# A three-engine hand-over in a four-layer kernel: GpSimd's scales and weight pieces at other places, statistics buffers of their own, first pairs shared with ScalarE

## The chip, the cores and the metric

The kernel runs on one core of a Trainium2 chip. Its time is device time in microseconds, the median of several executions; lower is better. Five engines work side by side and are ordered by semaphores alone: TensorE (PE) multiplies, VectorE (DVE), ScalarE (ACT) and GpSimd (POOL) do everything between the matmuls, and SyncE (SP) issues the transfers. Every engine carries out its own instructions in the order in which the kernel lists them; an instruction whose semaphore isn't there holds back all that stand behind it on that engine.

## The reference

Four layers on x of shape 8 x 256 x 256 (batches, tokens, features), each with a layer norm ahead of it and a residual around it:

```python
x = x + attention(layernorm(x))   # 16 heads in 4 groups, causal, softmax, projection
x = x + ternary_linear(layernorm(layernorm(x), gamma, beta))  # weights -1, 0, 1
x = x + linear_attn(layernorm(x))
x = x + gated_ffn(layernorm(x))

# linear_attn: Q, K, V = split(X W_in + b_in); Q, K get a rotary embedding
A = sum over tokens of (K / |K|) * V
Y = (A * Q) W_out + b_out
# and adds the normalised X itself

# gated_ffn: integer weights minus 128, times a scale per row
out = (silu(x Wg) * (x Wu)) Wd
```

All values are float32. Products are made of rounded float32 parts: an operand is split into a high part (the rounded copy) and a low part (what is left), and most products are three matmuls: high by high, high by low, low by high. So nearly every tile is needed twice, as a high half that ScalarE copies out of the matmul's bank and as a low half that VectorE gets by a subtraction.

## The kernel before

**Stages.** The eight batches of 256 tokens go through attention one after the other (`batch(n, last)` on every engine; n = 0 is written out, 1 to 6 are a loop, 7 is written out). Within a batch, j counts 8 pairs of heads. The ternary layer of batch n - 1 and the statistics for the linear layer lie within the attention of batch n; the ternary layer of the last batch lies within the linear layer. That layer is `linear(n)` for n = 1 to 7, all written out, and the gated layer is `gated(m, ...)` over four pairs of batches with six tiles of the hidden dimension each, in a loop for the middle two. The opening (before `batch(0, False)`) is an order written out by hand, since the weights arrive meanwhile.

**A pair of heads.** TensorE makes the scores of pair j + 2 while the probabilities of pair j are transposed. VectorE's `row_max` adds the causal mask to the first 128 rows' diagonal block (line 1528), then takes sum and minimum in four custom reductions (line 1532). ScalarE's `exps` makes the exponentials with their row sums (line 1141). VectorE inverts the sums (line 1548); `normalise` multiplies the probabilities of head 0 on GpSimd (line 521) and of head 1 on VectorE (line 1557). For the very first pair VectorE also does the second rows of head 0 (line 1554). TensorE transposes them (lines 751 and 754), ScalarE and VectorE split them (`pT_hi`, line 1103, and `pT_lo`, line 1486), and `attend` and `out_project` use them. `q_hi`, `q_lo`, `v_hi`, `v_lo`, `o_hi` and `o_lo` split other tiles by the same two lines. `late_hi` and `late_lo` split weights in the first batch.

**GpSimd's other work.** It makes the low halves of the gated layer's weights in eight pieces (`gated_weights_lo`, line 538; GU0 and GU1 with four parts each), takes the variances to the power -1/2 (`inv_std`, `inv_std_twice`), makes the scales of the linear layer in seven small operations (`linear_scale(n)`, lines 490 to 499), adds bias rows to the residual (`add_row`, line 455: `linear_bias`, `ternary_bias`), and in the linear layer does the rotary embedding's sine products (line 468), the sums (lines 478 and 485) and the inverse norm of k (line 508), which ScalarE's `weigh` (line 1337) waits for.

**A step of the linear layer.** On TensorE, `linear(n)` is: k projection of batch n, output product of batch n - 2 (`linear_out`, line 940), transposes of the normalised batch n + 1 (line 659), `linear_sum(n - 1)` (line 927), q projection of batch n. VectorE applies the norm (`linear_apply`, line 1731), makes the q products (lines 1761 and 1764), copies k with its bias (line 1744), makes its cosine products (line 1752), adds the output product to x (`add_bank`, line 1720), splits the transposed tile (line 1486) and reduces the token sums to A (`linear_sum`, line 1776). ScalarE scales q by A to y (`linear_y`, line 1353). GpSimd's `q_rotate` and `k_inverse` stand between these. In step 2 VectorE normalises the last batch for the ternary layer (`ternary_apply`, line 1709) at the end; in steps 3 and 5 it splits the down projection's weights (line 1816).

**Hand-over.** The gated layer's first two batches are normalised within steps 7 and 8 of this order: `ln_moments` (lines 1469 and 1473) on VectorE, `inv_std` (lines 444 and 446) on GpSimd, `gated_apply` (line 1480), transposes, `gated_x_hi` and `gated_x_lo` (lines 1280 and 1830). All calls of `ln_moments` share the buffers `stats`, `moments`, `variance` and `rstd`, and are counted: call NB + b is the gated batch b. After the last step ScalarE does `linear_y(NB - 1)`, then the first silu (line 1390), before which an activation table is loaded. A flag that says whether any low half of the gated weights is other than zero is made of four sums (`sum_gated_lo`, `sum_down_lo`, line 1245, on ScalarE); it picks two matmuls instead of three per product in the gated layer of this run.

## Time and profile before

| what | value |
|---|---|
| median of 3 runs (lowest to highest) | 582.9 us (582.8 to 583.08) |
| the profiled execution's own time | 582.94 us |
| its span | 581.1 us |
| TensorE matmuls, weight loads | 564.4 us, 532.3 us |
| VectorE, ScalarE, GpSimd | 469.1 us, 370.8 us, 220.9 us |

The span runs from the first instruction of the program to the last one, and the time has 1.84 us around it. "Busy" means that an instruction of the engine was under way; the matmuls are pipelined, so TensorE's 564.4 us isn't TensorE at its peak. An idle piece of an engine is put down to the instruction whose semaphore came last. By the timeline the opening is 0 to about 60 us (the first batch), attention goes on until about 445 us, the linear layer's steps until about 504 us, the gated layer until about 574 us.

### The profile page before, as it was taken

How to read it: one execution, taken by the hardware profiler on the slowest of the kernel's cores; microseconds unless marked ns; L12 is line 12 of the kernel's file. 1: busy time of each engine (PE TensorE's matmuls, PEld its weight loads, DVE VectorE, ACT ScalarE, POOL GpSimd, SP SyncE). 2: the span in 40 equal slices, each digit the busy share in tenths (PEclk: the TensorE clock that was granted, in tenths of full speed). 3: DMA queues.
4: the chain of work that ended last, by engine and by line, in shares of the span. 5: the costliest groups of instructions: out<-in, count | busy, mean ns of one | idle time of the engine just before them, and what ended most of it. 6: DMA issues, size and time to landing. Idle time of an engine off the chain costs nothing.

```text
span 581.1 us, 12867 instructions
## 1 busy us (share of the span) xinstructions
PE 564.4 (97%) x4131; PEld 532.3 (92%) x4131; DVE 469.1 (81%) x1476; ACT 370.8 (64%) x1035; POOL 220.9 (38%) x325
## 2 busy tenths in 40 slices
PE   8899999999999999999999999999999898899995
PEld 8799999999999999999999999999998797788884
DVE  5789789778878987797789778977877997878875
ACT  5896656656755756576567657557877776654452
POOL 3773224233223422332233233323446798503320
PEclk9999999999999999999999999999999998999998
DMA  8806000000000000000000000000000000001001
GB/s 324 293 1 227 2 1 3 1 1 0 0 0 0 0 0 0 0 0 0 0 0 0 0 0 0 0 0 1 1 1 2 1 2 0 2 0 37 25 30 57
DMA packets 9152, 14.71 MB, mean 25 GB/s; under 512 B 1568, under 2 KB 6688, under 8 KB 9120
## 3 DMA queue, kind: packets, MB, share of 16 engines
q1 hardware_dynamic: 9120, 14.30, 6.9%
q8 instruction: 18, 0.29, 0.2%
q14 instruction: 14, 0.11, 0.1%
HBM read 12.20 MB, written 2.10 MB: 25 GB/s over the span
## 4 chain that ended last, share of the span: by engine, by line
PE 83%; DVE 7%; POOL 4%; ACT 3%; issue 2%; POOLq 0%; DVEq 0%; ACTq 0%
PE bank L649 67%; PE bank L735 5%; PE bank L751 5%; PE bank L754 2%; PE bank L659 2%; DVE raw L1764 1%; PE bank L864 1%; ACT prob L1141 1%; PE bank L1048 1%; POOL qkv L468 1%; POOL prob L508 1%; DVE prob L1532 1%; ACT raw L1330 0%; DVE raw L1761 0%; POOL qkv L485 0%
## 5 line engine op out<-in xcount | busy, mean ns | idle before, releaser
L521 POOL TENSOR_SCALAR prob<-prob,rowinv 128x256 f32<-128x256 f32 (+1 forms) x127 | 96.3, 771 | 273.3 <-DVE rowinv L1548 273.3
L649 PE MATMUL bank<-xT,big 128*128 128x256 f32 x984 | 129.7, 284 | 0.1
L649 PEld LDWEIGHTS bank<-xT,big 128*128 128x128 f32 x984 | 123.4, 192 | 1.0 <-issue 0.2
L1141 ACT ACTIVATE prob<-prob,negmax 128x128 f32<-128x128 f32 (+1 forms) x256 | 112.8, 444 | 9.5 <-DVE negmax L1532 9.5
L649 PE MATMUL bank<-wp,oT 128*128 128x256 f32 x768 | 102.5, 283 | 0.2
L649 PEld LDWEIGHTS bank<-wp,oT 128*128 128x128 f32 x768 | 96.8, 190 | 1.2 <-DVE oT L1486 0.7
L1103 ACT ACTIVATE qT<-bank 128x512 fp32r<-128x512 f32 x68 | 40.6, 597 | 72.8 <-PE bank L649 72.7
L649 PE MATMUL bank<-pT,v 128*128 128x512 f32 (+1 forms) x384 | 80.0, 343 | 0.1
L649 PEld LDWEIGHTS bank<-pT,v 128*128 128x128 f32 x384 | 63.1, 189 | 9.5 <-issue 0.5
L1486 DVE TENSOR_TENSOR pT<-bank,pT 128x512 fp32r<-128x512 f32 (+1 forms) x128 | 65.1, 550 | 3.1 <-ACT pT L1103 3.0
L1103 ACT ACTIVATE pT<-bank 128x512 fp32r<-128x512 f32 (+1 forms) x128 | 55.2, 483 | 12.1 <-PE bank L751 10.0
L1486 DVE TENSOR_TENSOR qT<-bank,qT 128x512 fp32r<-128x512 f32 x68 | 46.8, 688 | 16.7 <-ACT qT L1103 16.7
L1486 DVE TENSOR_TENSOR oT<-bank,oT 128x512 fp32r<-128x512 f32 x64 | 44.0, 688 | 15.7 <-ACT oT L1103 15.0
L649 PE MATMUL bank<-kT,qT 128*128 128x256 f32 x384 | 56.2, 282 | 0.0
L649 PEld LDWEIGHTS bank<-kT,qT 128*128 128x128 f32 x384 | 50.2, 190 | 0.0
L1532 DVE CUSTOM_DVE_ANT_0 prob<-bank,mask 128x256 f32<-128x256 f32 x128 | 48.6, 416 | 0.0
L1141 ACT ACTIVATION_READ_ACCUMULATOR prob<-prob,negmax 128x1 f32 x256 | 48.5, 190 | 0.0
L735 PE MATMUL bank<-kT,qT 128*128 128x256 f32 x256 | 46.1, 302 | 1.5 <-DVE negmax L1532 1.2
L649 PE MATMUL bank<-wp,big 128*128 128x512 f32 (+1 forms) x176 | 45.3, 398 | 0.8 <-DVE wp L1830 0.7
L1103 ACT ACTIVATE oT<-bank 128x512 fp32r<-128x512 f32 x64 | 37.2, 581 | 4.4 <-PE bank L649 4.4
L751 PE MATMUL bank<-ident,prob 128*128 128x128 f32 x256 | 38.3, 272 | 0.0
L649 PEld LDWEIGHTS bank<-wp,big 128*128 128x128 f32 x176 | 31.6, 189 | 7.1 <-DVE wp L1830 1.1
(180 smaller groups left out, 965.1 us busy)
## 6 DMA issues: line engine op xcount, KB each, us to landing
raw<-in_wq SPq DMA_DIRECT2D x4, 512.0 KB, 7.0
raw<-in_wp SPq DMA_DIRECT2D x4, 512.0 KB, 7.3
x<-in_x SPq DMA_DIRECT2D x7, 256.0 KB, 7.0
out<-x SPq DMA_DIRECT2D x7, 256.0 KB, 2.1
raw<-in_w_gu SPq DMA_DIRECT2D x2, 640.0 KB, 5.1
raw<-in_w_in SPq DMA_DIRECT2D x1, 768.0 KB, 4.6
raw<-in_w_down SPq DMA_DIRECT2D x1, 640.0 KB, 6.8
raw<-in_wk SPq DMA_DIRECT2D x1, 512.0 KB, 3.8
```

The lines of the kernel that those rows point to most:

```text
L468: m = pool.tensor_tensor(k_sin[q][:, :, e, :], k[:, :, 1 - e, :], sin[:, :, e, :], ALU.mult)
L508: pool.tensor_tensor(xw[n % 2][:, :, D:D + 1], k_bound[:, :].rearrange("p (t o) -> p t o", o=1), exponent[:, 0:ST].rearrange("p (t o) -> p ...
L521: m = pool.tensor_scalar(prob[:, j % 2, 0, a:b], prob[:, j % 2, 0, a:b], rowinv[:, j % 2, r:r + 1], None, ALU.mult)
L649: m = pe.matmul(out, lhs(a), rhs(b), start=first and i == 0, stop=last and i == len(passes) - 1, skip_group_check=True)
L659: m = pe.transpose(out[:, k * S + t * P:k * S + (t + 1) * P], src[:, t, k * P:(k + 1) * P], ident[:])
L735: m = pe.matmul(bS0[:, i * S:(i + 1) * S], qT[:, a, i, 0:P], kT[:, :, g, 0:P], start=a == 0, stop=a == 1, skip_group_check=True)
L751: m = pe.transpose(bT0[:, i * S + r * P:i * S + (r + 1) * P], prob[:, j % 2, i, r * P:(r + 1) * P], ident[:])
L754: m = pe.transpose(bT1[:, i * P:(i + 1) * P], prob[:, j % 2, i, 2 * P:3 * P], ident[:])
L1103: act.activation(out, src, ACT.Copy).then_inc(done, 1)
L1141: m = act.activation(prob[:, j % 2, i, a:b], prob[:, j % 2, i, a:b], ACT.Exp, scale=-1.0, bias=negmax[:, 2 * i + r:2 * i + r + 1], accum_o ...
L1486: dve.tensor_tensor(out, src, f32(hi), ALU.subtract).then_inc(done, 1)
L1532: return dve.tensor_tensor_reduce(prob[:, j % 2, i, a:b], src, other, -SCALE, -MASKED, ALU.add, ALU.min, negmax[:, 2 * i + r:2 * i + r + 1])
```

## The change

GpSimd: all four pieces of GU0 are made at j = 4 of the last attention batch, and after them the linear scales of batch 6 (before: two pieces there, two more at j = 6, the scales in step 3 of the linear layer). Three pieces of GU1 follow at j = 6 (before: one there, two in step 4); the fourth stays in step 5. The scales of batch 7 move from the start of step 5 to the end of step 4. The statistics for these scales move with them on VectorE: those of batch 6 go from step 2 to j = 5 of the last attention batch.

Second gated batch: its statistics use the buffers of the ternary layer (`t_stats`, `t_moments`, `t_variance`, `t_rstd`), which are free by then, in functions of their own, at the end of step 6; its normalisation moves into step 7, ahead of `linear_sum(6)`; TensorE transposes it ahead of `linear_sum(7)`. VectorE's tail after step 7 has another order, and the shared calls are renumbered. The ternary normalisation of step 2 moves from the end to after the q products.

Opening: ScalarE normalises head 1 of the first pair and splits its transposed probabilities ahead of the exponentials of pair 1. VectorE's `row_max` is in two functions, and the first (the masked add) of pairs 1 and 2 stands ahead of an inversion.

Tail: both multiplications of the last batch's scales stand ahead of both adds.

```diff
 # GpSimd
+            def gated_inv_std():
+                pool.wait_ge(s_fvar, NB + 1)
+                pool.tensor_tensor(t_rstd[:, :], t_variance[:, :], exponent[:, 0:ST], ALU.pow).then_inc(s_frs, 1)
 # batch(n, last)
                         if j == 4:
-                            gated_weights_lo(GU0, 0)
-                            gated_weights_lo(GU0, 1)
+                            for part in range(4):
+                                gated_weights_lo(GU0, part)
+                            linear_scale(NB - 2)
                         if j == 6:
-                            gated_weights_lo(GU0, 2)
-                            gated_weights_lo(GU0, 3)
-                            gated_weights_lo(GU1, 0)
+                            for part in range(3):
+                                gated_weights_lo(GU1, part)
 # linear(n)
-                if n == 5:
-                    linear_scale(NB - 1)
                 if n > 0:
                     q_rotate(n - 1)
...
-                if n >= NB - 2:
-                    inv_std(n + 2)
+                if n == NB - 2:
+                    inv_std(NB)
...
-                if n == 3:
-                    linear_scale(NB - 2)
                 if n == 4:
-                    gated_weights_lo(GU1, 1)
-                    gated_weights_lo(GU1, 2)
+                    linear_scale(NB - 1)
                 if n == 5:
                     gated_weights_lo(GU1, 3)
+                if n == NB - 2:
+                    gated_inv_std()
 # TensorE, linear(n)
                 if n == NB - 1:
+                    gated_transpose(1)
                     linear_sum(n)
-                    gated_transpose(1)
                     linear_out(n - 1)
 # ScalarE
+            def normalise_first():
+                act.wait_ge(s_ri, 1)
+                for r, (a, b) in enumerate(((0, P), (P, 3 * P))):
+                    m = act.activation(prob[:, 0, 1, a:b], prob[:, 0, 1, a:b], ACT.Copy, scale=rowinv[:, 0, 2 + r:3 + r])
+                m.then_inc(s_pn1, 1)
...
+                if n == 5:
+                    sum_down_lo(1)
                 if n == NB - 2:
                     sum_gated_lo(GU1)
-                    sum_down_lo(1)
...
             v_hi(0, 0)
+            normalise_first()
             late_hi(3)
             q_hi(0, 2)
+            pT_hi(0, 0)
             exps(0, 1)
 # VectorE: row_max(n, j) is now row_max_first(n, j), the masked add, and
 # row_max_rest(n, j), the four reductions
             q_lo(0, 1)
+            row_max_first(0, 1)
             invert_sums(0, 0)
             normalise(0, 0)
             v_lo(0, 0)
-            row_max(0, 1)
+            row_max_rest(0, 1)
             q_lo(0, 2)
+            pT_lo(0, 0, 0)
+            pT_lo(0, 0, 1)
+            row_max_first(0, 2)
             invert_sums(0, 1)
             normalise(0, 1)
             batch(0, False)
 # in batch(0) at j == 0: row_max_rest(0, 2) ahead of q_lo(0, 3), in place of
 # row_max(0, 2) behind it
 # batch(n, last) at j == 5
                             linear_apply(1)
                             o_lo(n, j)
+                            linear_moments(NB - 2)
 # linear(n)
                     q_products(n - 1)
+                    if n == 2:
+                        ternary_apply(NB - 1)
...
-                    if n >= NB - 2:
-                        ln_moments(n + 2, n + 2 - NB)
+                    if n == NB - 2:
+                        ln_moments(NB, 0)
                     add_bank(n - 2, bY, s_lo, s_lres, s_la)
                     linear_x_lo(n + 1, (n + 1) % 2) if n + 1 < NB else gated_x_lo(0)
+                    if n == NB - 1:
+                        gated_apply(1)
                     linear_sum(n - 1)
...
-                if n == 2:
-                    ternary_apply(NB - 1)
-                    linear_moments(NB - 2)
...
+                if n == NB - 2:
+                    gated_moments()
                 if n == NB - 1:
-                    gated_apply(1)
 # after step 7
+            gated_x_lo(1)
+            linear_sum(NB - 1)
             q_products(NB - 1)
-            linear_sum(NB - 1)
-            gated_x_lo(1)
 # tail
             for t in range(ST):
                 dve.tensor_tensor(scaled[1][:, t, :], ...)
+            for t in range(ST):
                 dve.wait_ge(s_gsc, b + t + 1)
                 dve.tensor_tensor(x_tile(b, t), x_tile(b, t), scaled[1][:, t, :], ALU.add).then_inc(s_gl, 1)
```

`gated_moments()` is `ln_moments` and the variance plus epsilon for batch 1 with the ternary buffers: two `bn_stats`, two `bn_aggr` and one `tensor_scalar`.

## Rows read from the trace of the kernel before

**Rows 1.** The page: each engine's busy time, its share of the span, instructions

```profile
PE 564.4 (97%) x4131; PEld 532.3 (92%) x4131; DVE 469.1 (81%) x1476; ACT 370.8 (64%) x1035; POOL 220.9 (38%) x325
```

**Rows 2.** Waits of TensorE: who for whom, us in total, times, longest

```profile
PE bank L940 <- ACT raw L1353: 2.2, 1, 2.2
...
PE bank L659 <- DVE y L1709: 1.8, 1, 1.8
PE bank L735 <- DVE negmax L1532: 1.2, 1, 1.2
PE bank L649 <- DVE wp L1830: 0.7, 1, 0.7
PE bank L659 <- DVE xn L1480: 0.5, 1, 0.5
```

**Rows 3.** Windows of 4 us: stretch, busy by engine, clock, DMA share, GB/s

```profile
484.00:488.00 4.00, 3.32 (x8) 2.56 (x9) 3.94 (x6) 1.97 (x5) 2.38 (x3) 0.62 0.00 0
```

**Rows 4.** Timeline of the opening: start, us, engine, line, tiles, idle before

```profile
16.26 0.49 ACT L1141 ACTIVATE prob<-prob,negmax 128x256 f32<-128x256 f32 x1
...
18.24 0.72 DVE L1557 TENSOR_SCALAR prob<-prob,rowinv 128x128 f32<-128x128 f32 x2
...
26.20 0.41 DVE L1528 TENSOR_TENSOR prob<-bank,mask 128x256 f32<-128x256 f32 x1
...
27.87 0.71 PE L735 MATMUL bank<-kT,qT 128*128 128x256 f32 x4 [1.20 <-DVE negmax L1532]
```

**Rows 5.** Timeline of the last attention batch

```profile
430.90 1.86 POOL L538 TENSOR_TENSOR big<-raw,big 128x352 fp32r<-128x352 f32 x2
...
433.06 0.73 DVE L1731 TENSOR_SCALAR xn_b<-x,linear_negated_mean,linear_rstd 128x256 f32<-128x256 f32 x2
...
435.47 1.02 DVE L1486 TENSOR_TENSOR pT<-bank,pT 128x512 fp32r<-128x512 f32 x2 [1.08 <-ACT pT L1103]
...
437.70 0.66 DVE L1557 TENSOR_SCALAR prob<-prob,rowinv 128x128 f32<-128x128 f32 x2
437.76 1.65 POOL L521 TENSOR_SCALAR prob<-prob,rowinv 128x128 f32<-128x128 f32 x2 [5.00 <-DVE rowinv L1548]
```

**Rows 6.** Timeline of the linear layer's steps

```profile
458.79 0.74 DVE L1676 BATCH_NORM_STATS2 linear_stats<-x 128x6 f32<-128x256 f32 x2
...
458.95 1.29 POOL L455 TENSOR_TENSOR x<-x,biases 128x512 f32<-128x512 f32 x1 [0.56 <-DVE y L1709]
...
459.74 0.98 DVE L1731 TENSOR_SCALAR xn<-x,linear_negated_mean,linear_rstd 128x256 f32<-128x256 f32 x2
...
474.29 0.89 ACT L1353 ACTIVATE raw<-qkv,A_sb 128x256 f32<-128x256 f32 x2
...
474.84 1.67 DVE L1731 TENSOR_SCALAR xn<-x,linear_negated_mean,linear_rstd 128x256 f32<-128x256 f32 x2
...
475.36 1.89 PE L940 MATMUL bank<-raw 128*128 128x256 f32 x8
...
483.97 1.93 DVE L1731 TENSOR_SCALAR xn_b<-x,linear_negated_mean,linear_rstd 128x256 f32<-128x256 f32 x2 [1.64 <-ACT prob L1337]
...
484.68 3.55 PE L940 MATMUL bank<-raw 128*128 128x256 f32 x8 [2.17 <-ACT raw L1353]
```

**Rows 7.** Timeline of the hand-over to the gated layer

```profile
492.13 1.60 DVE L1480 TENSOR_SCALAR xn<-x,moments,rstd 128x256 f32<-128x256 f32 x2 [0.86 <-POOL rstd L446]
...
502.34 0.98 DVE L1764 SCALAR_TENSOR_TENSOR raw<-bank,q_bias,rope 64x256 f32<-64x256 f32 x2
...
504.19 0.91 ACT L1353 ACTIVATE raw<-qkv,A_sb 128x256 f32<-128x256 f32 x2 [1.18 <-DVE A_sb L1776]
...
510.61 0.68 DVE L1851 TENSOR_TENSOR kT<-raw,kT 128x512 fp32r<-128x512 f32 x1
...
512.13 1.12 PE L649 MATMUL bank<-big,kT 128*128 128x256 f32 x8
```

**Rows 8.** Timeline of the tail

```profile
574.96 1.25 DVE L1983 TENSOR_TENSOR x<-x,qkv 128x256 f32<-128x256 f32 x1
```

More of the change, by code:

```diff
@@ L1577, in batch @@
                     if first:
+                        row_max_rest(n, 2)
                         q_lo(n, 3)
-                    if j < J - 2 or not last:
+                    elif j < J - 2 or not last:
                         row_max(*ahead(n, j, 2))
@@ L1981, in _ @@
                 dve.tensor_tensor(scaled[1][:, t, :], bD[1][:, t * D:(t + 1) * D], biases[:, 2, :], ALU.mult).then_inc(s_gsc, 1)
+            for t in range(ST):
                 dve.wait_ge(s_gsc, b + t + 1)
```

37 lines of the change are left out of this document (30 added, 7 removed).

## The prediction

> **What bounds the kernel now.** I read the page's busy times first: TensorE has work under way for 564.4 us of a span of 581.1 [rows 1], so a change that takes no matmul away can only win what TensorE waits. The waits of TensorE come next [rows 2]: 2.2 us in one piece for ScalarE's scaled y, 1.8 for VectorE's ternary xn, 1.2 for a row maximum in the opening, 0.7 for the low half of a transposed tile and 0.5 for a normalised tile at the hand-over to the gated layer; that for the constants at the start, which the change doesn't touch, and pieces under 0.3 us are left out here. Then the windows: after the 2.2 us wait the granted clock is 0.62 over 484 to 488 us, that is the 1.2 GHz level for most of that stretch, against 1.00 elsewhere [rows 3]. The reader sees the price beside it: the same eight matmul instructions take 3.55 us there and 1.89 one layer step earlier [rows 6], so the wait costs 2.2 + 1.7 = 3.9 us, and 0.2 more in the transposes behind it. The 1.8 us wait left the clock alone. Everything together is 6.4 us of waits and 1.9 us of clock, about 8.3 us, and the timeline around each wait says who is late. All steps are set against this execution: 582.94 us, 1.84 around its span; the median of the runs is 582.9, so nothing is to be shifted.
>
> **Opening (first pairs).** Removed from VectorE's path: the two normalisations of pair 0's second head, 0.72 us, and the masked add of 0.41 us in each of two row maxima, which moves into time in which VectorE waited for exponentials. Added to ScalarE: the same two normalisations; its exponential of the wider shape takes 0.49 us, so both some 0.8 to 0.9 us [rows 4]. VectorE reaches the second row maximum about 1.1 us sooner. The query tile of pair 2 now hangs on ScalarE, which does it after the normalisations and a weight copy: it comes 0.3 to 0.5 us sooner at most, and the exponentials of pair 1 start some 0.3 us later than at present. Following the order from there (low halves of pair 0's transposes, inversion, normalisation, v, then the rest of the third row maximum, 1.2 us of four reductions), the maximum that began at 26.20 is complete near 25.8 instead of 27.7, and TensorE's scores at 27.87 wait for the low half of the fourth query tile, near 26.5. TensorE's own work would let it start there at 26.5. Bounds: 0.2 us, if ScalarE's queue is what ends last, and 1.4, the wait with the sliver before it. I take 1.2, for VectorE's row is the one that ended last.
> The Trainium skill (Perfetto Trace Analysis, Optimizing Scalar/DVE Operations) holds that an operation which either engine can do is faster on VectorE where a performance mode exists, and that one moves it only if VectorE is saturated. The rows agree on the durations (0.72 against some 0.9) and not on the path: VectorE carries four tiles that TensorE waits for. By the rule the opening would give nothing, and the sum would be 1.2 us higher.
>
> **Last attention batch.** GpSimd stands idle for 5.00 us before its last normalisation at 437.76; two pieces of the gated weights take 1.86 us before that idle time [rows 5]. Two pieces more (1.9 us) and one set of linear scales (2.0) are put into it: 3.9 of 5.00 us. The scales wait for the moments of tile 6, which now stand on VectorE behind the normalised tile and the low half of o: 1.0 us, the pair of statistics as at 458.79 and a quarter for the aggregation [rows 6]. The idle time before VectorE's transposed probabilities at 435.47 is 1.08 us, so alone the moments would just fit. But VectorE's tensor_scalar on a 256-wide tile suffers from GpSimd's pieces: two take 0.73 us alone at 433.06 and 1.67 when they meet two pieces at 474.84 [rows 5, 6]. With the pieces 3 and 4 at 432.7 to 434.6, the three such operations at 432.8 to 433.8 lose 0.9 to 1.3 us. The probabilities then begin 0.9 to 1.3 us late, and TensorE's attend, which reads them, with them; short waits for VectorE in the same batch, under 0.3 us each, close in exchange. Behind the waiting scales on GpSimd is its last normalisation, which starts about 1.0 us late, when TensorE is late too. Bounds: 0 (the pieces don't meet those operations) and 1.3. I take +0.7.
> The Trainium skill (SBUF — State Buffer, Who interferes with whom) says that GpSimd and a two-port VectorE operation hold their shared ports for whole instructions and the other fully blocks. At 437.70 two VectorE normalisations lost only 0.12 us beside GpSimd's 1.65 us pair, so here the trace shows both behaviours. By full blocking this part costs 1.3, by the mild one 0.2.
>
> **Ternary layer's last tile.** VectorE's ternary normalisation moves ahead of k_copy, which takes away TensorE's 1.8 us wait. The tile steps behind it get later by 0.9 us (0.73 and one meeting with GpSimd's q_rotate). What is late next: GpSimd has two residual adds of 1.29 us one behind the other, the second no longer waiting for VectorE, and VectorE's linear_apply(4) meets both. It ends near 460.8, as now (459.74 + 0.98), and q products, k copy, k_squares, the transposed tile and the scaled y follow at today's times. TensorE's linear_out starts at 475.36 with y ready at 475.18 (474.29 + 0.89) [rows 6]; a TensorE that arrives 1.8 us early waits there instead. Bounds: 0 and -1.8. I take 0.
>
> **The wait for the scaled y.** Taken out of GpSimd's linear steps: two pieces (1.9 us by their length in [rows 5]) and one set of scales (some 2 us); the last set of scales follows the residual add directly. VectorE's apply at 474.84 then meets the add alone and gains 0.4 us. GpSimd's rotation, sine products and inverse, on which ScalarE's weighing and y wait, start 1.5 to 2 us sooner. y takes 0.89 us and ended with the wait, at 484.6; the queue gives it back 2.2 to 2.4 us, so it is ready near 482.3, and TensorE was free at 484.68 - 2.17 = 482.5 [rows 6]. So the 2.2 us wait and the 1.9 us of clock go, 4.1 us on TensorE. VectorE's chain, however, gains only what its next normalisation gains: it waited for the weighed x until 483.97 and then met an add and a piece (1.93 us) [rows 6]; the piece is still there, so it ends near 483.8 instead of 485.9, 2.1 us sooner. TensorE waits on that chain at the next k projection and y. Bounds: -2.1 (VectorE's chain decides) and -4.1 (TensorE decides). I take -2.1, because VectorE, ScalarE and GpSimd hand each tile around within one layer step and the margin at 475.36 was 0.2 us.
>
> **Second gated batch and hand-over.** The statistics of batch 1 (1.2 us on VectorE, 0.7 on GpSimd) move into VectorE's 0.86 us wait before 492.13; the normalisation there was held up to 1.60 us by an add and loses its excess, so they cost nothing [rows 7]. The normalisation of batch 1 moves ahead of linear_sum(6), and TensorE transposes it ahead of linear_sum(7). This takes away the waits of 0.5 and 0.3 us, and the low half that ended the 0.7 us wait comes 2.4 us sooner. What is late next is the tail: q products (0.98 us for two of three instructions, 1.45 for all) now stand behind the low half of the second transposed tile and the last linear_sum, so they and GpSimd's rotation (0.75) put the last y at about 505.5 in today's frame instead of 504.19. Behind y on ScalarE are the activation table's load and the first silu, and behind these the first low half of the hidden tile, which ends at 511.3, 7.1 us after y's start; TensorE's first down projection at 512.13 needs it [rows 7]. 505.5 + 7.1 = 512.6, so y's delay comes out there at +0.5 us net. Bounds: -1.5 (the waits just go) and +1.3 (y's whole delay). I take +0.5.
>
> **Tail.** The multiplication of the last tile runs beside the first add (1.25 us, slowed by GpSimd) instead of behind it: 0.41 us of multiplication leaves the end, of which the store's issue can use 0.2 to 0.4 [rows 8]. I take -0.3. The lo sum moved a step earlier on ScalarE finds its input ready and lies in idle time, and GpSimd's renumbered calls change no work: 0.
>
> **Sum.** -1.2 + 0.7 + 0 - 2.1 + 0.5 - 0.3 = -2.4 us: 582.94 - 2.4 = 580.5 us. Its own range, from the bounds that don't need another mechanism: 579.0 to 582.0.
>
> **Rivals.**
> (a) TensorE decides, not the chain of the other three. For it: VectorE is busy for 81% only, and two of its idle pieces in these steps are there because of the stalls themselves. Against it: the 0.2 us margin. Then -1.2 + 0.3 - 1.8 - 4.1 + 0 - 0.3 = -7.1: 575.8 us; halfway outcomes lie at 577 to 579.
> (b) The change gives nearly nothing: ScalarE becomes the bound of the opening (-0.2), the last batch costs its 1.3, the 2.2 us wait shrinks but reappears at the next y (-2.1), hand-over +0.5, tail 0: -0.5, 582.4 us. For it: ScalarE and VectorE are both full in the opening. Part of it is that the earlier statistics don't bring the second gated batch forward at all.
> (c) Slower. The one mechanism is VectorE's queue in the last batch: the moments that stand before the transposed probabilities. If the pieces and the statistics together hold the attend back by 2.2 us or more, the length of wait after which the clock fell at 484.68, the level of 1.2 GHz costs 1.9 on top, +4.1 in all. The other parts give -1.2 - 2.1 - 0.3 = -3.6, and the hand-over, whose last y hangs on the same VectorE, takes its upper bound of +1.3: 582.94 - 3.6 + 4.1 + 1.3 = 584.7 us. It decides from a wait of 2.2 us on; below that the sum stays under 582.94. Against it: I find 1.3 us at most for that wait.
>
> **Numbers.** Likeliest case 0.48, (a) with its halfway outcomes 0.27, (b) 0.15, (c) 0.10. A measurement of this kernel can tell a change of about 0.2%, 1.2 us, from none, so faster is below 581.7. The likeliest case gives 0.43 of that, (a) 0.27, (b) 0.02: faster 0.72. Slower is over 584.1: 0.08. Same 0.20. The range that holds it 8 times in 10 leaves out the slower case and the far end of (a): 576.5 to 582.8.
>
> **What would show it.** In the profile after, the wait of TensorE for VectorE's y near 459 is gone and a new one stands near the output product of step 5 (then 0 is right) or not (then (a)). The windows show a granted clock of 1.00 through the linear steps. The scores at 27.87 start near 26.6. In the last batch the attend that follows VectorE's row at 435.47 starts 0.9 to 1.3 us later against the projection before it, with VectorE's applies near 1.7 us instead of 0.73. The first down projection waits over 1 us, with the table load later against the gate projection than now. The prediction is wrong if the linear steps give over 4 us, or if the last batch costs over 1.5.

## Result and profile after

The changed kernel takes 580.42 us in the median of 5 runs (580.01 to 580.6); the kernel before takes 583.08 (582.8 to 583.26) beside it. The ratio is 0.9956, with an interval of 0.9944 to 0.9968. A second measurement on another chip gives 580.04 us and 0.9942 (0.9927 to 0.9957). The profiled execution has 580.42 us and a span of 578.6, so 2.5 us of span went.

The page of the changed kernel, busy times. TensorE does the same 4131 matmuls in 1.7 us less busy time than in [rows 1]; this is the clock, which had cost the output product of step 6 1.66 us (3.55 against 1.89 in [rows 6]). The other engines are where they were.

```profile
PE 562.7 (97%) x4131; PEld 530.6 (92%) x4131; DVE 469.3 (81%) x1475; ACT 370.7 (64%) x1037; POOL 220.5 (38%) x324
```

Waits of TensorE in the changed kernel (columns as in [rows 2]; the line numbers have moved, so L661 is L659 of before, L651 is L649):

```profile
PE bank L661 <- DVE xn L1865: 1.3, 1, 1.3
PE bank L651 <- DVE kT L1895: 1.2, 1, 1.2
PE bank L651 <- DVE qT L1498: 1.2, 2, 0.9
PE bank L651 <- DVE pT L1498: 1.2, 1, 1.2
PE bank L737 <- DVE qT L1498: 0.5, 2, 0.3
```

Four of the five waits of [rows 2] are gone. The fifth, 0.5 us for the second gated batch's xn, has grown to 1.3 at its new place, and two more single waits of over a microsecond have come, for kT and pT. All of them are for VectorE, and each is in a stage that the change gave more work or another order. The window in which the clock had been 0.62 [rows 3], and the stretch in which the output product of step 6 now lies, in the changed kernel:

```profile
484.00:488.00 4.00, 3.23 (x21) 2.81 (x19) 3.88 (x11) 1.70 (x6) 3.09 (x6) 1.00 0.00 0
...
480.00:484.00 4.00, 3.96 (x27) 3.38 (x26) 3.99 (x7) 3.49 (x9) 3.21 (x3) 1.00 0.00 0
```

To see where the 2.5 us come from, I compare the starts of the same TensorE instructions in both traces. "Against the loop" means: the shift of that start, less the shift of the transposes that stand at 289.75 us before and at 287.86 after, in the middle of the steady loop. This takes out the start of the execution, which scatters: the first transposes of probabilities (19.22 before, 19.06 after) lie between 18.70 and 20.02 us in the fourteen traces of this case. Every number in the table is the difference of two starts in the timelines.

| kernel | opening | attend, last batch | output product, step 5 | output product, step 7 | first down | last matmul | first transposes to last matmul |
|---|---|---|---|---|---|---|---|
| changed | -1.73 | +1.07 | +1.05 | -1.71 | -0.53 | -0.58 | -2.31 |
| changed, again (e7) | -1.73 | +1.04 | +1.01 | -1.76 | -0.59 | -0.73 | -2.46 |
| e1 opening only | -1.71 | -0.01 | +1.57 | -0.38 | +0.70 | +0.48 | -1.23 |
| e9 all but the opening | -0.02 | +1.06 | +1.06 | -1.74 | -0.56 | -0.65 | -0.67 |
| e2 ternary tile back | -1.72 | +1.08 | +0.95 | -2.28 | -1.11 | -1.26 | -2.98 |
| e3 weight pieces back | -1.72 | +1.06 | +1.06 | +0.10 | +1.28 | +1.14 | -0.58 |
| e4 tail order back | -1.72 | +1.09 | +1.03 | -1.76 | -1.82 | -1.91 | -3.63 |
| e5 statistics sooner | -1.73 | +0.12 | +0.10 | -2.67 | -1.49 | -1.63 | -3.36 |
| e6 pieces split | -1.72 | +0.51 | +0.62 | -2.17 | -0.98 | -1.10 | -2.82 |
| e8 two (e2, e4) | -1.74 | +1.07 | +0.96 | -2.29 | -2.35 | -2.46 | -4.20 |
| e10 three (e2, e4, e5) | -1.78 | +0.13 | +1.61 | -2.29 | -2.36 | -2.49 | -4.27 |
| e11 four (and e6) | -1.77 | +0.49 | +0.47 | -2.73 | -2.82 | -2.82 | -4.59 |
| e12 five | -1.75 | +0.48 | +2.03 | -1.89 | -2.66 | -2.80 | -4.55 |

The output products of steps 5, 6 and 7 are those that start at 475.36, 484.68 and 493.24 us in the kernel before. "Opening" is the shift of the loop against the first transposes; the last column is the opening and the last matmul together. The columns between are cumulative: the step from one to the next is the cost of the stage between them. For the changed kernel the stages are: opening -1.73, last attention batch +1.07, ternary tile -0.02, wait for y -2.76, hand-over +1.18, rest -0.05. The sum is -2.31; the first transposes were 0.16 sooner and the end behind the last matmul 0.04 shorter, which makes -2.51. Each row is one execution; the changed kernel's two agree within 0.15 us in every column.

The rows of the changed kernel behind these stages. Opening, answering to [rows 4]: the two normalisations that ScalarE took over, and the scores that stood at 27.87:

```profile
17.97 0.79 ACT L1152 ACTIVATE prob<-prob,rowinv 128x128 f32<-128x128 f32 x2
...
25.96 0.50 PE L737 MATMUL bank<-kT,qT 128*128 128x256 f32 x2 [0.32 <-DVE qT L1498]
```

Last attention batch, answering to [rows 5]:

```profile
429.01 3.74 POOL L543 TENSOR_TENSOR big<-raw,big 128x352 fp32r<-128x352 f32 x4
...
430.71 1.24 DVE L1578 TENSOR_SCALAR prob<-prob,rowinv 128x128 f32<-128x128 f32 x2
431.87 1.35 DVE L1754 TENSOR_SCALAR xn_b<-x,linear_negated_mean,linear_rstd 128x256 f32<-128x256 f32 x2
433.15 0.68 DVE L1498 TENSOR_TENSOR oT<-bank,oT 128x512 fp32r<-128x512 f32 x1
433.75 0.74 DVE L1699 BATCH_NORM_STATS2 linear_stats<-x 128x6 f32<-128x256 f32 x2
434.52 0.25 DVE L1704 BATCH_NORM_AGGREGATE linear_moments<-linear_stats 128x2 f32<-128x6 f32 x2
434.68 0.99 DVE L1498 TENSOR_TENSOR pT<-bank,pT 128x512 fp32r<-128x512 f32 x2
```

Two things stand ahead of the copy of pT: the statistics (433.75 to 434.68, 0.93 us), and the stretching of two pairs of VectorE's normalisations beside GpSimd's run of four pieces (1.24 and 1.35 us; the normalising pair takes 0.54 us at 432.61 before the change, the apply 0.73 in [rows 5]). Together 2.2 us; 1.08 us of idle time was there to take them. TensorE's attend at 435.49 waits 1.21 us.

Linear steps, answering to [rows 6]. The output product of step 6 starts without a wait, and TensorE waits later, at the k projection of step 7:

```profile
480.02 1.08 DVE L1841 SCALAR_TENSOR_TENSOR big<-raw,big 128x768 fp32r<-128x768 int32 x1
...
480.24 2.02 POOL L460 TENSOR_TENSOR x<-x,biases 128x512 f32<-128x512 f32 x1
...
481.02 2.34 DVE L1754 TENSOR_SCALAR xn_b<-x,linear_negated_mean,linear_rstd 128x256 f32<-128x256 f32 x2
...
481.40 1.97 PE L942 MATMUL bank<-raw 128*128 128x256 f32 x8
...
488.10 1.70 PE L651 MATMUL bank<-big,qT 128*128 128x256 f32 x12 [0.87 <-DVE qT L1498]
```

Hand-over, answering to [rows 7]: the last y, the load of the activation table behind it, the low half of the hidden tile and the first down projection:

```profile
502.56 0.91 ACT L1362 ACTIVATE raw<-qkv,A_sb 128x256 f32<-128x256 f32 x2 [3.66 <-POOL qkv L490]
...
503.49 1.28 ACT L1400 ACT_TABLE_LOAD   x1
...
508.98 0.68 DVE L1895 TENSOR_TENSOR kT<-raw,kT 128x512 fp32r<-128x512 f32 x1
...
509.71 1.22 PE L651 MATMUL bank<-big,kT 128*128 128x256 f32 x8 [1.24 <-DVE kT L1895]
```

Tail, answering to [rows 8]: both additions as one group, and the last stores on SP's queue; the last line is the second of the two stores in the line above it.

```profile
572.70 1.38 DVE L2032 TENSOR_TENSOR x<-x,qkv 128x256 f32<-128x256 f32 x2
573.49 0.37 SPq L421 DMA_DIRECT2D out<-x  x1
573.91 0.96 SPq L424 DMA_DIRECT2D out<-x  x2
574.42 0.44 SPq L424 DMA_DIRECT2D out<-x  x1
```

The same last store in the kernel before:

```profile
577.03 0.34 SPq L424 DMA_DIRECT2D out<-x  x1
```

### The profile page after: what moved, and what is told of

The parts are those of the page before. It is cut to its first block, busy times and chain, and to the rows that moved or that the text cites. A ratio compares the mean times of both kernels' runs of the same rounds, so it can differ in the third digit from the quotient of the medians.

```text
span 578.6 us, 12867 instructions
## 1 busy us (share of the span) xinstructions
PE 562.7 (97%) x4131; PEld 530.6 (92%) x4131; DVE 469.3 (81%) x1475; ACT 370.7 (64%) x1037; POOL 220.5 (38%) x324
## 4 chain that ended last, share of the span: by engine, by line
PE 80%; DVE 10%; ACT 5%; issue 3%; POOL 1%; DMA 0%; DVEq 0%; SPq 0%; POOLq 0%
PE bank L651 65%; PE bank L737 5%; PE bank L753 4%; PE bank L756 2%; PE bank L661 2%; ACT prob L1143 1%; PE bank L866 1%; DVE raw L1787 1%; DVE xn_b L1754 1%; DVE prob L1552 1%; DVE qkv L1767 1%; ACT raw L1339 1%; DVE pT L1498 1%; ACT big L1116 0%; DVE oT L1498 0%
## 5 line engine op out<-in xcount | busy, mean ns | idle before, releaser
L651 PE MATMUL bank<-xT,big 128*128 128x256 f32 x984 | 129.7, 284 | 0.1
L651 PEld LDWEIGHTS bank<-xT,big 128*128 128x128 f32 x984 | 123.4, 192 | 1.0 <-issue 0.3
L651 PE MATMUL bank<-wp,oT 128*128 128x256 f32 x768 | 102.5, 283 | 0.3 <-DVE oT L1498 0.3
L651 PEld LDWEIGHTS bank<-wp,oT 128*128 128x128 f32 x768 | 96.8, 190 | 1.1 <-DVE oT L1498 0.5
L651 PE MATMUL bank<-pT,v 128*128 128x512 f32 (+1 forms) x384 | 79.8, 343 | 1.2 <-DVE pT L1498 1.2
L651 PEld LDWEIGHTS bank<-pT,v 128*128 128x128 f32 x384 | 63.2, 189 | 10.2 <-issue 1.4
L651 PE MATMUL bank<-kT,qT 128*128 128x256 f32 x384 | 56.2, 282 | 0.0
L651 PEld LDWEIGHTS bank<-kT,qT 128*128 128x128 f32 x384 | 50.2, 190 | 0.0
L651 PE MATMUL bank<-wp,big 128*128 128x512 f32 (+1 forms) x176 | 45.3, 398 | 0.1
L651 PEld LDWEIGHTS bank<-wp,big 128*128 128x128 f32 x176 | 31.6, 188 | 6.2 <-issue 0.3
```

The costliest lines, as they stand in the source:

```text
L651: m = pe.matmul(out, lhs(a), rhs(b), start=first and i == 0, stop=last and i == len(passes) - 1, skip_group_check=True)
```

## Experiments

Each kernel was timed in five rounds beside the kernel before; e1 to e4 share a chip, e5 to e8 another, e9 to e12 a third. The kernel before has 583.25, 583.16 and 582.95 us on them, and times from different chips are compared by their ratios to it. The changed kernel has 0.9956 and 0.9942. Only e4 and e12 have intervals wholly below both of its intervals, and only e3 and e9 wholly above; e8 and e10 lie below the first alone. The other kernels can't be told from the changed one by time, and what is said of them rests on one trace each.

**The opening: alone (e1), and everything without it (e9).** e1 is the kernel before with the opening's edits alone:

```diff
 # kernel before, all else as it was
+            normalise_first()            # ScalarE
+            pT_hi(0, 0)
+            row_max_first(0, 1)          # VectorE, ahead of invert_sums(0, 0)
+            row_max_first(0, 2)          # VectorE, ahead of invert_sums(0, 1)
```

> The kernel before with the opening's edits alone. Theory 1 (the opening is worth what TensorE's offset against the kernel before shows in the steady loop of the changed kernel, 1.9 us, and all of it reaches the end): 581.2 us, span 579.2. Rival, the prediction's term of 1.2: 581.9. Rival 2 (a gain in the opening is given back later, at the waits of the linear layer): within 0.3 us of before.

579.99 us (578.94 to 582.19), ratio 0.994 (0.9925 to 0.9955); its profiled execution is the slowest of its runs, 582.19. The opening gives 1.71 us there, as theory 1 has it, all of it kept through the loop and the last batch. The median is 1.2 us below theory 1's 581.2, and why isn't shown. By its ratio the opening alone can't be told from the whole change: the rest of the change adds only -0.58 us in the table. Then comes the wait for the ternary y, and in this execution the clock falls behind it. TensorE's timeline and then the windows there, in e1 (0.56 is mostly the level of 1.2 GHz):

```profile
457.50 0.66 PE L659 MATMUL bank<-ident,y 128*128 128x128 f32 x4 [1.82 <-DVE y L1728]
457.92 2.62 PE L649 MATMUL bank<-big,qT 128*128 128x256 f32 x12
```

```profile
458.00:460.00 2.00, 2.00 (x13) 2.00 (x12) 1.95 (x7) 1.77 (x4) 0.81 (x1) 0.56 0.00 0
460.00:462.00 2.00, 2.00 (x8) 1.71 (x8) 1.95 (x4) 0.87 (x2) 1.23 (x1) 0.58 0.00 0
```

In the kernel before the same wait of 1.8 us left the clock alone. So one execution of e1 says little of the parts behind that point, and its other runs, down to 578.94, are not those of the trace.

e9 is the other side:

```diff
 # changed kernel
-            normalise_first()
-            pT_hi(0, 0)
-            row_max_first(0, 1) ... row_max_first(0, 2)
```

> The changed kernel without the opening's edits (no normalising on ScalarE, no row maxima in halves, pT of the first pair back in the batch's loop); all else of the change stays. Theory 1: the opening's 1.7 us carry through to the end, for TensorE has no slack in the steady loop and the tail follows it: 1.6 to 1.9 us above the changed kernel, 581.7 to 582.3 us. Theory 2: the linear steps are set by the other engines' chain, which doesn't begin sooner with the loop; then part of the opening's gain is lost in the waits of the last batch and the linear steps, and the kernel without it is at most 0.8 us above the changed one, 580.8 to 581.2 us.

581.89 us (580.45 to 582.69), ratio 0.9981 (0.9971 to 0.999). In the table it is the changed kernel in every column between the first and the last, to within 0.1 us. The opening's 1.7 us reach the last matmul whole (572.52 against 570.83); theory 1 holds. e1 and e9 take the opening's edits as one: what ScalarE's two normalisations and what the split row maxima give alone was not run.

**The ternary tile (e2).**

```diff
                     q_products(n - 1)
-                    if n == 2:
-                        ternary_apply(NB - 1)
...
+                if n == 2:
+                    ternary_apply(NB - 1)
                 if n == 3:
```

> The changed kernel with the ternary normalisation of the last batch back at the end of step 2. Theory 1 (its move only shifts TensorE's wait of 1.8 us to later places, since the output product of step 5 is bound by the chain of VectorE, ScalarE and GpSimd): no more than 0.3 us slower than the changed kernel, 580.4 to 580.7, with TensorE's wait near 457 back at 1.8 to 2.0 us and the output product of step 5 where it is now (474.5). Rival (TensorE decides): 1.8 us slower, 582.2.

579.14 us (578.52 to 580.61), ratio 0.9935 (0.9919 to 0.995). TensorE's wait for y is back, 1.80 us at 457.65, and yet at the output product of step 5 both kernels stand at the same place (+0.95 and +1.05). So the move gives nothing by then, as theory 1 has it, and by step 7 it costs 0.6 us (-2.28 against -1.71), which neither theory had. The clock didn't fall behind the wait in this execution. The 0.6 us are in VectorE's chain from step 3 on. In the changed kernel the apply of step 3 stands beside two residual adds of GpSimd that follow each other at once (first two lines), in e2 it doesn't wait and meets less of them (third line):

```profile
457.37 2.58 POOL L460 TENSOR_TENSOR x<-x,biases 128x512 f32<-128x512 f32 x2
457.79 2.31 DVE L1754 TENSOR_SCALAR xn<-x,linear_negated_mean,linear_rstd 128x256 f32<-128x256 f32 x2 [0.44 <-ACT prob L1346]
```

```profile
457.51 1.71 DVE L1754 TENSOR_SCALAR xn<-x,linear_negated_mean,linear_rstd 128x256 f32<-128x256 f32 x2
```

Against the loop the apply ends 0.54 us sooner in e2 (459.22 against 460.10), and the apply of step 6 still starts 0.56 us sooner (480.12 against 481.02). TensorE feels it only where it waits for VectorE again, behind the output product of step 5.

**The weight pieces and scales in steps 4 and 5 (e3).**

```diff
                         if j == 6:
-                            for part in range(3):
-                                gated_weights_lo(GU1, part)
+                            gated_weights_lo(GU1, 0)
 # linear(n)
+                if n == 5:
+                    linear_scale(NB - 1)
...
                 if n == 4:
-                    linear_scale(NB - 1)
+                    gated_weights_lo(GU1, 1)
+                    gated_weights_lo(GU1, 2)
```

> The changed kernel with two of GU1's pieces back in GpSimd's step 4 and the scales of batch 7 back at the start of step 5. Theory 1 (this edit ends the wait for y and its fall of the clock, of which VectorE's chain passes on 2.8 us): 583.2 us, a wait of 2 us or more at the output product of step 6 and a granted clock under 0.8 in the 4 us around it. Rival (the new place of the scales of batch 6 and of the first pieces already suffices): 580.4 to 581.2, clock 1.00.

582.29 us (580.71 to 582.75, 11 runs), ratio 0.9979 (0.9969 to 0.9989): over half of the change's gain is gone with this one part, near theory 1. The wait is back, and of full length (e3's timeline and window):

```profile
483.92 1.99 PE L944 MATMUL bank<-raw 128*128 128x256 f32 x8 [2.17 <-ACT raw L1364]
```

```profile
484.00:488.00 4.00, 4.00 (x21) 3.53 (x22) 3.90 (x9) 2.77 (x8) 2.38 (x5) 1.00 0.00 0
```

The product takes 1.99 us, not the 3.55 of [rows 6]: behind the same 2.17 us wait the clock stayed up in this execution, against theory 1. The execution is the fastest of e3's eleven, 1.6 us below their median; whether the clock fell in the others isn't shown. It prices the part without its clock: from the output product of step 5 to that of step 7 the changed kernel gains 2.76 us on the kernel before, and e3 still 0.96. So this part is worth 1.8 us without the clock. The other 1.0 us is put down to the clock, which fell in the kernel before and not in e3; no run has that alone.

**The order of VectorE's tail behind step 7 (e4).**

```diff
+            q_products(NB - 1)
             gated_x_lo(1)
             linear_sum(NB - 1)
-            q_products(NB - 1)
```

> The changed kernel with VectorE's last q products ahead of the low half of the second gated tile and of the last linear_sum, as before the change; nothing else. Theory 1 (the late y delays the table load, the first silu, the first low half and so the first down projection, where TensorE waits 1.2 us): that wait goes, 579.2 to 579.6 us. Rival (TensorE waits elsewhere in the hand-over, for the second transposed tile): 580.4, with the wait moved ahead of the gate projections.

578.25 us (577.43 to 579.93), ratio 0.991 (0.9896 to 0.9924). The wait of 1.2 us at the first down projection is gone, and it starts 1.3 us sooner (-1.82 against -0.53 in the table), because the last y does:

```profile
501.71 0.91 ACT L1362 ACTIVATE raw<-qkv,A_sb 128x256 f32<-128x256 f32 x2 [2.41 <-PE bank L942]
```

The rest of the hand-over loses nothing; theory 1 holds, and the time is 1 us below its 579.2 to 579.6.

**The last attention batch: the queue or GpSimd (e5, e6).** e5 takes the statistics out of the way:

```diff
                         if j == 3:
                             linear_apply(0)
+                            linear_moments(NB - 2)
...
                             linear_apply(1)
                             o_lo(n, j)
-                            linear_moments(NB - 2)
```

> The changed kernel with linear_moments(NB - 2) of the last attention batch made at its fourth pair, behind linear_apply(0), instead of at its sixth behind linear_apply(1) and o_lo. Theory 1 (queue): in the changed kernel's profile VectorE spends about 0.98 us on these statistics (433.75 to 434.75) ahead of the copy of pT that the attend at 435.49 waits for 1.21 us, so the wait falls to below 0.5 us, attend(6) starts 0.7 to 1.2 us sooner against the steady loop, and the last matmul 0.7 to 1.0 us sooner; time 579.4 to 579.7 if the changed kernel is at 580.4. Theory 2 (GpSimd): what delays VectorE there is the run of four weight pieces on GpSimd, which stretches whatever VectorE does; then the wait at attend(6) keeps more than 0.8 us and the time stays within 0.3 us of the changed kernel.

579.02 us (578.87 to 579.54), ratio 0.9932 (0.992 to 0.9945). The attend waits 0.29 us and starts 0.95 us sooner against the loop, with VectorE's two stretched pairs as long as they were (1.24 and 1.35); that is theory 1. e6 takes the pieces away from these instead:

```diff
+                        if j == 3:
+                            for part in range(2):
+                                gated_weights_lo(GU0, part)
                         if j == 4:
-                            for part in range(4):
+                            for part in range(2, 4):
                                 gated_weights_lo(GU0, part)
```

> The changed kernel with the first two of the four weight pieces GU0 issued at the fourth pair of the last attention batch and the other two with the scale at the fifth, instead of all four at the fifth. Theory 1 (queue): VectorE's statistics ahead of the copy of pT set the wait of 1.21 us at attend(6); moving pieces takes at most 0.3 to 0.6 us from it (the normalising pair and the apply, 1.24 and 1.35 us each beside the pieces and 0.54 and 0.73 us in the kernel before), time 0 to 0.5 us below the changed kernel. Theory 2 (GpSimd): the two normalisings and the apply come back to 0.54 and 0.73 us, VectorE is 1.1 us earlier, the wait at attend(6) all but goes and the time is 0.8 to 1.2 us below the changed kernel.

579.83 us (579.42 to 580.63), ratio 0.9949 (0.9936 to 0.9962). VectorE in e6:

```profile
430.75 0.91 DVE L1581 TENSOR_SCALAR prob<-prob,rowinv 128x128 f32<-128x128 f32 x2
431.58 0.72 DVE L1757 TENSOR_SCALAR xn_b<-x,linear_negated_mean,linear_rstd 128x256 f32<-128x256 f32 x2
```

The apply is back at its old length and the statistics still stand ahead of pT, yet the wait is down to 0.14 us too. The two causes are both real and neither theory is right alone: 0.93 us of statistics and 1.3 us of stretching met 1.08 us of slack, and to take away the one, or 0.96 us of the other as e6 does, is enough. But in e6 the transposes before that attend are 0.52 us late against the loop already (0.00 in the changed kernel), so the earlier pieces give half of it back. By time e6 can't be told from the changed kernel beside it (e7, 580.04 us).

**The changed kernel again (e7).**

> The changed kernel itself, beside the others on this chip. From its first measurement 0.9956 of the kernel before: 579.9 to 581.2 us. If the clock of TensorE falls behind its waits in some executions only, its runs spread less than those of the kernel before, since its waits in the linear steps are all below 1.5 us.

580.04 us (578.72 to 580.57). Its trace repeats the first one within 0.1 us in all columns up to the first down projection. The spread of 1.9 us is less than the 2.5 of the kernel before on this chip (581.41 to 583.95), but over 6 runs against 11, and in the first measurement it was 0.6 us against 0.5: the expectation on the spread is not shown.

**Together (e8, e10, e11, e12).** e8 is e2's and e4's edit.

> The changed kernel with two of its edits undone: ternary_apply(NB - 1) back at the end of the third linear step, and q_products(NB - 1) back ahead of gated_x_lo(1) and linear_sum(NB - 1). Theory 1: each undoes a loss of its own (0.7 and 1.4 us by the last matmul against the loop) and they lie in different stages, so they add: last matmul 2.1 us sooner than the changed kernel against the loop, 578.0 to 578.8 us. Theory 2: the chain of the other engines takes up what TensorE wins at the ternary tile (a second limit behind it), so that together they give no more than the tail order alone, 1.4 us: 578.9 to 579.4 us.

578.64 us (577.03 to 579.3), ratio 0.992 (0.9904 to 0.9935). Last matmul -2.46 against -0.58: 1.88 us, where the two alone give 0.68 and 1.33. They add, to within 0.13 us; the trace is for theory 1, the time, whose interval reaches into both theories' ranges, for neither.

e10 adds e5's edit to these, e11 adds e6's to the three.

> The changed kernel with three edits: ternary_apply(NB - 1) back at the end of the third linear step, q_products(NB - 1) back ahead of gated_x_lo(1) and linear_sum(NB - 1), and linear_moments(NB - 2) at the last batch's fourth pair. Theory 1 (waits in different stages add): 0.9 us less than the two alone, last matmul 3.0 us sooner than the changed kernel against the loop, 577.2 to 577.9 us. Theory 2 (a second limit behind): no more than 0.3 us less than the two, 578.3 to 578.9 us.

> The three edits before this, and the weight pieces GU0 split over the fourth and the fifth pair of the last batch. Each of the two edits in that batch alone took the wait at attend(6) from 1.21 us to about 0.3. Theory 1 (one wait, two causes of which either is enough): together they give no more than one, within 0.3 us of the three edits. Theory 2 (two costs that add): 0.6 to 0.9 us less than the three edits, 576.4 to 577.2 us.

e10: 578.13 us (577.19 to 579.58), ratio 0.9923 (0.9907 to 0.994). e11: 579.15 us (577.47 to 579.84), ratio 0.993 (0.9913 to 0.9947). Neither can be told from e8, or from the other, by its time. In the table e10 gains the 0.94 us at the attend and loses more behind the wait for y, where its clock fell; e8's did not, behind a wait as long. TensorE's timeline in e8, then in e10, then the windows of e10; in e8 both windows have a clock of 1.00:

```profile
457.98 0.66 PE L661 MATMUL bank<-ident,y 128*128 128x128 f32 x4 [1.83 <-DVE y L1732]
458.39 1.68 PE L651 MATMUL bank<-big,qT 128*128 128x256 f32 x12
459.91 1.89 PE L942 MATMUL bank<-raw 128*128 128x256 f32 x8
```

```profile
457.69 0.66 PE L661 MATMUL bank<-ident,y 128*128 128x128 f32 x4 [1.83 <-DVE y L1732]
458.10 2.45 PE L651 MATMUL bank<-big,qT 128*128 128x256 f32 x12
460.35 2.75 PE L942 MATMUL bank<-raw 128*128 128x256 f32 x8
```

```profile
458.00:460.00 2.00, 2.00 (x15) 2.00 (x13) 1.99 (x3) 1.59 (x4) 1.10 (x1) 0.67 0.00 0
460.00:462.00 2.00, 2.00 (x7) 1.69 (x7) 1.92 (x4) 1.05 (x3) 1.23 (x1) 0.50 0.00 0
```

At the output product of step 7 both stand at -2.29: TensorE's later wait for qT, 0.8 us in e8, is 0.17 in e10 and takes the loss in. In e11, whose clock stayed up, e5's edit and e6's together give 0.44 us over e8 at step 7. So theory 1 of e10 (0.9 us more) is not seen in one execution with a fallen clock, and can't be told by the times; for e11 theory 1 (one wait, either cause is enough) is what the attend shows: +0.49, no sooner than with e6 alone, and 0.36 us later than in e10, which has e5's edit without e6's.

e12 moves the second gated batch's normalisation ahead of the copy that follows ScalarE's wp:

```diff
+                    if n == NB - 1:
+                        gated_apply(1)
                     linear_x_lo(n + 1, (n + 1) % 2) if n + 1 < NB else gated_x_lo(0)
-                    if n == NB - 1:
-                        gated_apply(1)
```

> The four edits before this, and in the last linear step gated_apply(1) ahead of gated_x_lo(0) instead of behind it. Theory 1 (queue): VectorE stands 0.40 us in its queue for ScalarE's wp and then copies wp for 0.69 us ahead of the normalising of the second gated batch, whose result TensorE waits for 1.3 us; ahead of it the result is there 1.0 us sooner, the wait falls to 0.3 us or less, and the time is 0.6 to 1.0 us less than with four edits. Theory 2: TensorE's time is only passed on to the gates, whose weight-sized copy wp now comes 0.6 us later (a new wait at gate(0,0) of 0.5 us or more): the time stays within 0.3 us of the four edits.

577.65 us (575.47 to 578.91), ratio 0.9899 (0.9882 to 0.9917): the lowest median of all, 1.5 us under e11, though its interval overlaps those of e4, e8, e10 and e11. VectorE and TensorE in e12:

```profile
494.85 0.73 DVE L1868 TENSOR_SCALAR xn<-x,ternary_moments,ternary_rstd 128x256 f32<-128x256 f32 x2
495.50 0.68 DVE L1877 TENSOR_TENSOR wp<-bank,wp 128x512 fp32r<-128x512 f32 x1
...
496.33 0.63 PE L664 MATMUL bank<-ident,xn 128*128 128x128 f32 x4 [0.46 <-DVE wp L1877]
```

TensorE's wait falls from 1.3 us to 0.46 and another of 0.23, and the gates start without one. In this execution the clock fell once more behind the wait for y (+2.03 at step 5), and at the output product of step 7 e12 is 0.84 us behind e11; yet the last matmul came out level with e11's; its fastest run, with a span of 573.6, had a granted clock of 0.999 over the span where the profiled one had 0.995. So the normalisation's new place is worth about 0.8 us by the trace, nearer theory 1. What the five are worth with the ternary tile in its new place, where no wait of 1.8 us is left for the clock to fall behind, was not run.

## Why the prediction was right

The forecast was 580.5 us and the measured 580.42, with the forecast's signs in every stage that it gave one. The mechanisms held in the main, but the closeness of the number is luck: stage by stage the forecast missed by -0.5, +0.4, 0.0, -0.7, +0.7 and +0.3 us, and these errors cancel to 0.1. By term:

- **Opening: -1.2 forecast, -1.73 measured, outside the bounds given.** The order was right: ScalarE's pair takes 0.79 us, and the scores of 27.87 start at 25.96. The size was short because I counted one wait and left the small ones out. From start to start in the two timelines, 0.87 us of the gain lies at these scores. Of the rest, 0.38 us was gained by the scores of 21.65 and 0.50 in pieces from there to the end of the attend of 24.55. "TensorE's own work would let it start there at 26.5" was wrong for that reason: it arrived at 25.6 (25.96 less the wait of 0.32). The Trainium skill (Perfetto Trace Analysis, Optimizing Scalar/DVE Operations) speaks of offloading for a saturated VectorE, and of breaking up instructions for one that isn't saturated but makes other engines idle; that a move gives nothing otherwise was the prediction's reading of it. With VectorE at 81% of the span, a move and two broken-up row maxima gave 1.73 us together; no run here tells the two apart.
- **Last attention batch: +0.7 forecast, +1.07 measured, mechanism right.** The two stretched pairs lose 0.70 and 0.62 us, as in the upper bound. Full blocking, the rule of the Trainium skill (SBUF — State Buffer, Who interferes with whom), was the better description of GpSimd's pieces: the forecast had 1.3 by it and 0.2 by the mild row, and the pairs lost 1.32. The mild one was for GpSimd's scalar operation, L521, and I should not have averaged over two kinds of instruction. e5 shows that the moments, which I let "just fit", fit only where nothing else uses the slack. The short waits that were to close in exchange gave back 0.14 us.
- **Ternary tile: 0 forecast, -0.02 by step 5.** The 2.1 us by which TensorE's transposes of y came sooner (456.02 against 458.93, and +1.07 ahead of them) were given back as told, though not in one wait near the output product of step 5: 0.6 us by the first output product behind them, 0.6 by the second and 0.9 by the third. e2 shows what I missed: a further 0.6 us lost by step 7. In the list of stages these lie in the wait for y. I had the apply of step 3 end "as now", and in this it was nearly right (0.2 us late against the attend's shift), but without the move it would have ended 0.54 us sooner, since the statistics are no longer ahead of it.
- **Wait for the scaled y: -2.1 forecast, -2.76 measured, within the bounds.** Wait and fall of the clock are gone, and e3 shows that the pieces and scales were the cause of the wait. Part of it is VectorE's split of the down weights: before, it met the inverse of k's norm on GpSimd and stretched it to 1.51 us; now the inverse is done ahead of it, in 0.71 (478.87). That VectorE's chain takes part back is right as well: TensorE has gained 3.8 us by the transposes at 483.41, and 1.0 of them is lost by the k projection at 488.10, with its wait of 0.87 us. The mis-sized step is this one: the chain took 1.3 us of the 4.1, not 2.0. It did so although the apply came no sooner than forecast: it ends at 483.36 against 485.90, of which 0.82 us is the shift that the attend already had, so 1.7 us belong to this stage and not 2.1; it met a stretched residual add and takes 2.34 us, not 1.93. TensorE had more slack to this chain than I gave it: before, the low half of qT was done at 490.58 and TensorE came for it at 491.80.
- **Hand-over: +0.5 forecast, +1.18 measured.** The step from the last y to the first down projection was 7.1 us as forecast (502.56 to 509.71, 7.15). The last y was the mis-sized term: put into the kernel before's times by the 3.60 us that the output product of step 7 had gained, it starts at 506.16, not 505.5. e4, 1.29 us sooner at the first down projection, shows that the place of the q products is the whole of the loss there. "This takes away the waits of 0.5 and 0.3 us" was wrong for the first: TensorE waits 1.26 us for that tile at 496.74, since VectorE normalises it behind the copy of wp; e12 takes 0.8 us of this away.
- **Tail: -0.3 forecast, -0.04 measured, outside the bounds.** Behind the last matmul, which is 2.47 us sooner, the additions end 0.45 us sooner still (574.08 against 577.00), and the last store is issued 0.14 us sooner (574.42 against 577.03). Before, it followed the last addition by 0.03 us; now it stands behind the issue ahead of it on SP, which ends at 574.38. So SP's own issues hide two thirds of what VectorE wins. The end of the span shows 0.04 us of it, which one execution can't tell from the scatter of the ends.

The rivals: (a), that TensorE decides, is out at the ternary tile; at the y TensorE kept 2.76 of its 4.1 us. Its sum counts the last batch at +0.3, which the prediction doesn't derive; it was +1.07. (b) is out with the opening. (c) needed a wait of 2.2 us in the last batch; it was 1.21, and the clock stayed at 1.00. Of (c) the runs correct one thing, told below: 2.2 us is neither enough for a fall of the clock in every execution nor needed.

## What to carry to other kernels

A wait that is removed pays only down to the next engine's chain: look up who is late one product later before you count it. Where GpSimd gets a longer run of two-input operations, count a loss for each VectorE normalisation that meets it (0.6 to 0.7 us for a pair here), and put nothing else into the same slack; in the last batch either cost alone left a wait of 0.3 us or less. Sum the small waits of an opening: here they were half of its gain. And undo the parts of a change one by one even when its total is as forecast: by the last matmul the opening and the pieces gave 1.7 us each here, while the tail's order lost 1.3, the place of the statistics 1.0 and the ternary tile's 0.7.

## What the runs showed of the hardware

- **The fall of the clock is a matter of the execution.** Behind a 1.8 us wait for y it fell in e1, e10 and e12 and not in the kernel before, e2, e8 and e11; behind a wait of 2.17 us it fell in the kernel before and not in e3. The code at this wait is the same in the kernel before and e1. Where it falls it costs 1.6 us at once (by the next sum, in step 3, e1 stands at +1.57, after -0.01 ahead of the wait), part of which later waits take in. What decides isn't shown. A wait of this length is a risk, not a price, and one trace can't tell what its removal is worth. The Trainium skill (TensorE: Matmul & The Clock Gate, What's actually happening) says that the monitor doesn't start with the kernel, so that the point of change varies; no run here shows that cause.
- **GpSimd is stretched as well.** Its residual add takes 1.29 us in [rows 6] and 2.02 us at 480.24, where it starts 0.22 us behind VectorE's two-input operation of 768 elements. In e3 and in the kernel before, the same operation of VectorE meets the inverse instead, 1.51 us for 0.71.
- **Both ends of an execution scatter.** From the start of the last group of matmuls to the end of the span it is 7.4 to 8.1 us in eleven of the traces and 6.1 to 6.3 in e3, e9 and e10, with the same two groups of stores on SP. With the start's 1.3 us this is more than most edits here are worth; the starts of TensorE's instructions against the loop repeat to 0.15 us in the changed kernel's two traces and tell them apart.
